# Attention values by 32-column groups, sums from a block of ones, and 1024-column steps on VectorE and ScalarE

## The reference

```python
qh, kh, vh = (split_heads(qp), split_heads(kp), split_heads(vp))
scores = jnp.einsum('bhqd,bhkd->bhqk', qh, kh) * d_head ** (-0.5)
m = mask[:, None, None, :] | causal[None, None, :, :]
scores = scores - m.astype(scores.dtype) * NEG
attn = jax.nn.softmax(scores, axis=-1)
out = jnp.einsum('bhqk,bhkd->bhqd', attn, vh)
out = out.transpose(0, 2, 1, 3).reshape(b, l, d_model)
return out @ Wo.T + bo
```

## Time and profile before

| | us |
|---|---|
| median of 3 runs (763.24 to 767.15) | 765.07 |
| the profiled execution, its own time | 765.94 |
| its span, from the first to the last instruction | 763.8 |
| TensorE busy, of the span | 574.9 |
| VectorE busy | 443.1 |
| ScalarE busy | 407.7 |

### The profile page before, as it was taken

The page is one execution under the profiler, slowest core; times in us unless marked ns, Lnnn a source line. Parts: engine busy times, 40 slices in busy tenths (PEclk is TensorE's granted clock), DMA queues, the critical chain, the costliest instruction groups (busy, mean ns, idle before and its releaser), DMA issues.

```text
span 763.8 us, 14153 instructions
## 1 busy us (share of the span) xinstructions
PE 574.9 (75%) x4326; PEld 405.7 (53%) x4326; DVE 443.1 (58%) x1706; ACT 407.7 (53%) x862; POOL 359.7 (47%) x438
## 2 busy tenths in 40 slices
PE   3499999889888988898898767483778866789800
PEld 1156666556455555555465446362667755679700
DVE  4267788778777877777785773251323322223374
ACT  2257988887787888688786655230322322224300
POOL 4122126644554564455435326647555555550075
PEclk9989999999999999999998987867898999989955
DMA  3363111221122122201111224324544444446498
GB/s 89 71 195 84 45 41 44 61 67 43 50 60 66 29 65 63 66 24 30 38 29 32 83 59 122 105 77 112 158 133 124 118 125 124 120 131 186 133 364 291
DMA packets 74458, 73.59 MB, mean 96 GB/s; under 512 B 22032, under 2 KB 61840, under 8 KB 74096
## 3 DMA queue, kind: packets, MB, share of 16 engines
q1 hardware_dynamic: 64160, 53.86, 26.8%
q0 software_dynamic: 8640, 18.37, 6.8%
q10 hardware_dynamic: 1584, 0.46, 0.2%
HBM read 44.99 MB, written 27.70 MB: 95 GB/s over the span
## 4 chain that ended last, share of the span: by engine, by line
PE 53%; ACT 14%; issue 13%; DVE 7%; another core or an unknown queue 4%; POOL 4%; SPq 2%; DMA 2%; ACTq 0%; POOLq 0%; DVEq 0%
PE bank L638 12%; PE bank L649 10%; PE bank L462 6%; PE bank L484 6%; DVE sm L890 3%; PE bank L466 3%; POOL gathered L1417 3%; PE bank L475 3%; PE bank L629 3%; ACT sm L717 2%; ACT pt L782 2%; ACT vx L709 2%; ACT rows L744 2%; PE bank L491 2%
## 5 line engine op out<-in xcount | busy, mean ns | idle before, releaser
L1354 POOL DMA_INDIRECT routed_rows<-rows,pos x128 | 125.2, 978 | 136.4 <-ACT rows L746 86.2
L1390 POOL DMA_INDIRECT expert_rows_by_token<-yb,token_row x118 | 113.2, 960 | 85.7 <-DVE token_row L1248 40.8
L638 PE MATMUL bank<-xbT,wi 128*128 128x256 f32 x312 | 97.1, 439 | 71.1 <-issue 70.4
L827 ACT ACTIVATE hb<-bank 128x512 f32<-128x512 f32 x78 | 46.6, 597 | 168.7 <-PE bank L638 77.4
L1254 DVE TENSOR_TENSOR yb<-bank,gate 128x256 f32<-128x256 f32 x78 | 33.1, 424 | 172.2 <-PE bank L649 107.2
L638 PEld LDWEIGHTS bank<-xbT,wi 128*128 128x128 f32 x312 | 59.6, 212 | 84.7 <-issue 77.0
L882 DVE TENSOR_REDUCE smax<-bank 128x8 f32<-128x512 f32 x128 | 82.2, 683 | 30.7 <-PE bank L466 25.4
L649 PE MATMUL bank<-wo,hb 128*128 x624 | 91.6, 295 | 0.0
L649 PEld LDWEIGHTS bank<-wo,hb 128*128 128x128 f32 x624 | 85.3, 212 | 0.1
L462 PE MATMUL bank<-kx,qT 64*64 64x512 f32 x512 | 74.6, 654 | 14.0 <-DMA kx<-kT 7.1
L890 DVE TENSOR_TENSOR sm<-bank,smax 128x512 f32<-128x512 f32 x128 | 81.9, 681 | 0.0
(11 more groups left out here) (135 smaller groups left out, 934.8 us busy)
## 6 DMA issues: line engine op xcount, KB each, us to landing
xb<-routed_rows SPq DMA_DIRECT2D x78, 138.0 KB
wi<-w_in SPq DMA_DIRECT2D x78, 128.0 KB
kx<-expert_rows_by_token SPq DMA_DIRECT2D x26, 256.0 KB
ctx_in<-ctx_t SPq DMA_DIRECT2D x16, 256.0 KB
x_all<-x SPq DMA_DIRECT2D x16, 256.0 KB
kx<-kT SPq DMA_DIRECT2D x256, 16.0 KB
out<-x_all SPq DMA_DIRECT2D x16, 256.0 KB
expert_rows<-yb SPq DMA_DIRECT2D x19, 128.0 KB, 2.1
```

Of the source, the lines that this page charges most:

```text
L638: last = nc.tensor.matmul(UBK[b % 2][:, c * BLK:(c + 1) * BLK], wi[:, b % RX, c * P:(c + 1) * P], xbT[:, b % RH, :], start=True, stop=True)
L1354: nc.gpsimd.indirect_dma_start(out=rows_d, out_offset=bass.IndirectOffsetOnAxis(ap=pos[:, buf, k, u:u + 1], axis=0), in_=rows[:, buf, u, : ...
L1390: nc.gpsimd.indirect_dma_start(out=tok_d, out_offset=bass.IndirectOffsetOnAxis(ap=token_row[:, b % RY, u:u + 1], axis=0), in_=yb[:, b % RY ...
```

## The change

Six things change.

1. The products with the values and the sums. The stationary operands are now blocks of 32 columns. For each j in 0, 1 (head pair 2g+j), each sequence b and each g in 0 to 3 one product of a 128x32 block of `vx` with 64 moving columns (the queries of sequence b) adds into partitions 32g to 32g+31, columns 64b to 64b+63 of XB: 16 products a tile. The block has zeros for the heads of the other j, so that the two add up to the attention output with its 128 features on the partitions, which is the form that `project_o` takes. Eight more products of a 128x32 block of ones and zeros with 128 moving columns put each head's sum beside it, repeated over the head's 8 partitions (columns 128 to 255). So a tile has 24 products instead of 8.
2. With that, `queries_to_rows` (4 transposes), `transpose_o` (1 transpose), the evacuation `xo` and the evacuation `onT` go. `normalise(t)` reads XB itself: one reciprocal of 128 columns and one product of 128 columns, written to `onT` (two buffers).
3. `row_maxima`, `subtract_maxima`, `exps` and the evacuation of transposed exponentials are one instruction of 1024 columns each instead of two of 512. The score banks and the probability banks are now two tensors of 1024 columns over two banks each, and `s_sc`, `s_sub`, `s_exp`, `s_pt`, `s_ptev` count once a tile.
4. `values(t)` waits for `normalise(t-1)` (`s_norm`), since that reads XB.
5. `vx` has two buffers, is set to zero at the start (5,120 elements per partition, in place of four copies of 512), and `v_evac(s)` waits for the products of step s-2.
6. The buffer for gathered rows lies in `sm` and has 8 places instead of 6.

```diff
-VM = 64
+VB = 32
-RG = 6
+RG = 8
...
-        vx = sb("vx", [P, U, J, VM])
+        vx = sb("vx", [P, 2, U * J // 2, 2, 2 * VB + 2 * DH])
-        xo = sb("xo", [P, 4, P])
-        rden = sb("rden", [P, J, 2])
-        on = sb("on", [P, D])
-        onT = sb("onT", [P, P])
+        rden = sb("rden", [P, P])
+        onT = sb("onT", [P, 2, P])
...
                     if not first:
-                        pe.wait_ge(s_sub, 2 * t)
+                        pe.wait_ge(s_sub, t)
...
                 def values(t, u):
-                    pe.wait_ge(s_ptev, 2 * t + 2)
-                    for j in range(J):
-                        o = VM * (j % 2)
-                        last = nc.tensor.matmul(XB[o:o + VM, (j // 2) * P:(j // 2 + 1) * P], vx[:, u, j, :],
-                                                pt[:, j, :], start=True, stop=True)
+                    if t:
+                        pe.wait_ge(s_norm, t)
+                    pe.wait_ge(s_ptev, t + 1)
+                    for j in range(2):
+                        for b in range(2):
+                            for g in range(J // 2):
+                                v = vx[:, t // U % 2, u * (J // 2) + g, :, :].rearrange("p a c -> p (a c)")
+                                c = (2 * j + b) * VB
+                                nc.tensor.matmul(XB[g * VB:(g + 1) * VB, b * L:(b + 1) * L], v[:, c:c + VB],
+                                                 pt[:, 2 * g + j, b * L:(b + 1) * L], start=(j == 0 and b == 0), stop=False,
+                                                 skip_group_check=True)
+                    for j in range(2):
+                        for g in range(J // 2):
+                            last = nc.tensor.matmul(XB[g * VB:(g + 1) * VB, P:2 * P],
+                                                    ones_s[:, j * VB:(j + 1) * VB], pt[:, 2 * g + j, :],
+                                                    start=False, stop=(j == 1), skip_group_check=True)
                     last.then_inc(s_pv, 1)
-                def queries_to_rows(t):
...
-                def transpose_o(t):
...
                 def project_o(t):
-                    pe.wait_ge(s_ontev, t + 1)
-                    nc.tensor.matmul(YB[:, P:2 * P], onT[:, :], wo_s[:, :], start=True, stop=True).then_inc(s_y, 1)
+                    if t:
+                        pe.wait_ge(s_res, t)
+                    pe.wait_ge(s_norm, t + 1)
+                    nc.tensor.matmul(YB[:, 0:P], onT[:, t % 2, :], wo_s[:, :], start=True, stop=True).then_inc(s_y, 1)
...
                 def v_evac(s):
                     act.wait_ge(s_v, s + 1)
+                    if runs(s, 2):
+                        act.wait_ge(s_pv, (s - 1) * U)
...
                 def exps(t, u):
-                    for half in range(2):
-                        act.wait_ge(s_sub, 2 * t + half + 1)
-                        heads = sm[:, u % 2, half * HH:(half + 1) * HH, :]
-                        nc.scalar.activation(heads, heads, ACT.Exp).then_inc(s_exp, 1)
+                    act.wait_ge(s_sub, t + 1)
+                    nc.scalar.activation(sm[:, u % 2, :, :], sm[:, u % 2, :, :], ACT.Exp).then_inc(s_exp, 1)
...
                 def row_maxima(t):
+                    dve.wait_ge(s_sc, t + 1)
+                    nc.vector.reduce_max(smax[:, :], S2[:, :].rearrange("p (h k) -> p h k", k=L), AX).then_inc(s_max, 1)
...
                 def normalise(t):
-                    dve.wait_ge(s_tq, t + 1)
-                    y = YB[:, :].rearrange("r (j m) -> r j m", m=VM)
-                    nc.vector.reciprocal(rden[:, :, :], y[:, :, 4 * DH:4 * DH + 2]).then_inc(s_rden, 1)
+                    if t > 1:
+                        dve.wait_ge(s_y, t - 1)
+                    dve.wait_ge(s_pv, t + 1)
+                    nc.vector.reciprocal(rden[:, :], XB[:, P:2 * P]).then_inc(s_rden, 1)
                     dve.wait_ge(s_rden, t + 1)
-                    for b in range(2):
...
+                    nc.vector.tensor_tensor(onT[:, t % 2, :], XB[:, 0:P], rden[:, :], ALU.mult).then_inc(s_norm, 1)
...
-                for u in range(U):
-                    last = nc.vector.tensor_copy(vx[:, u, :, :], ones_s[:, :].unsqueeze(1).broadcast_to([P, J, VM]))
-                last.then_inc(s_zero, 1)
+                nc.vector.memset(vx[:, :, :, :, :], 0.0).then_inc(s_zero, 1)
```

122 lines of the change are left out of this document (43 added, 79 removed).

## The result

The changed kernel takes 796.5 us (median, 793.87 to 799.14) against 764.2 us (762.14 to 767.15) for the kernel before: a ratio of 1.044, 95% interval 1.040 to 1.049. The forecast was 750 us and faster; the range ended at 782. The profiled execution has a span of 794.9 us, against 763.8.

The account below looks back on a forecast made before the run. No engine was full; VectorE's and TensorE's rings were near the bound, VectorE last after the change. Savings of 0.9 us a step, 14.4 for 16 steps, 16.4 with the end, took 765.94 to 749.5, about 750 us; range 731 to 782.

Parts of the forecast that it names:

- the stall at u = 0: VectorE's 2.85 us idle before the residual ending u = 0: taken as external and staying, with 0.55 us a step saved there.
- VectorE's ring: Residual, subtraction, normalisation, small work, next maxima: +0.27 us a tile plus 0.05 handoff; last at u = 1, 2, level at u = 3.
- No dearer than the 1.02 before: Products with the values on TensorE: 48 records, four at once, taken as 1.05 us a tile against 1.02 before.
- Rival 3: Values on TensorE: the 48 records don't run four at once, 1.68 or 3.06 us; about 781 or 870 us; chance 0.17.
- the added wait: TensorE's values waiting for the previous tile's normalisation: 0 to 0.2 us, with slack for VectorE at u = 1 and 2.
- 0.9 us in each of 16 steps: Attention part: 0.35 us from three turns plus 0.55 at u = 0, 14.4 us in all; 16.4 with the end.
- The reciprocal: Normalisation on VectorE: a 128-column reciprocal taken as 1.0 us, making normalisation 1.33 us, 0.45 more a tile.
- rival 1: Normalisation: the reciprocal is as cheap as a product (0.29 us), TensorE's ring sets all turns; about 736 us; chance 0.16.
- Maxima and differences: VectorE's instructions of 1024 columns: 1.20 us each against 1.29 for two halves, saving 0.18 us a tile in all.
- The windows: Residual-to-residual turns of one attention step of four tiles, 25.8 us, to become 24.9; VectorE idle 0.55 us at u = 1.
- VectorE is last: Attention turns: VectorE sets the pace at u = 1 and 2 and is level at u = 3, saving 0.35 us together.
- the sign that would refute the prediction: Before VectorE's residuals: idle time there would show the forecast wrong; none was expected at u = 1, 2, 3.

Follow-up runs that it names:

- e5: The changed kernel with all eight scatters of a step waiting behind the output projections (three after u = 0, three after u = 1, two after u = 2): 736.6 us, ratio 0.954.
- e6: The kernel before with all eight scatters of a step moved behind the output projections, as in e5: 750.7 us, ratio 0.972.
- e9: e5 with two small VectorE routing steps rewritten (product L915 on ScalarE, copy L921 as a maximum over one element): 722.6 us, ratio 0.947.
- e10: e5 with the reciprocal computing 16 of 128 columns from the second tile on, output wrongly scaled: 721.3 us, ratio 0.944.
- e2: The kernel before with each product with the values cut into two of 64 columns, 32 records instead of 16, scatters in old places: 796.8 us, ratio 1.042.
- e4: The changed kernel with the scatter pairs of u = 1 and u = 2 waiting for that turn's output projection: 768.4 us, ratio 1.004.
- e11: The kernel before with every second product with the values cut into two of 64 columns, 24 records, scatters in old places: 784.2 us, ratio 1.029.

## Why the prediction was wrong

**Where it failed.** The step is the sentence on the stall at u = 0: "I take the stall to come from outside the five engines' work, and to stay." It came from one of the five, GpSimd, and it was not fixed to that turn: it belongs to scatters that meet a group of many short TensorE records. The rows for it were at hand: VectorE waited long after the recorded end of what it waited for, and GpSimd's four scatters filled the same 5 us. I looked at the DMA share of the window and didn't ask what GpSimd did. Had I, the next question would have been what stands beside the pairs at u = 1 and u = 2: the values, whose records the change triples. In the sum this is the term that stood at nothing: VectorE's ring has no idle time before the residuals at u = 1, 2 and 3, and the changed kernel waits there 1.17, 1.83 and 0.99 us on average.

**The values, priced right and still the cause.** "No dearer than the 1.02 before" holds: 1.02 from the first record to the projection. Rival 3 had the right place and sign with the wrong mechanism. The group doesn't take longer on TensorE; its notice comes 2 us later. In the sum this term had a width of 0 to 0.2 us a turn (the added wait) where u = 2 lost 1.65 in the sampled step and 1.40 on average.

**The rest of the sum,** with the holds gone (e5 against e6): 14.2 us saved, 16.4 predicted. That they are so close is mostly luck. The prediction put 0.9 us in each of 16 steps; over the 13 steps e5 saves 0.16 each. By the spans, of 12.8 us saved 7.1 lie ahead of the first expert product (427.5 against 434.6 us) and 5.7 behind it, where the prediction had nothing. In both kernels the stretched instructions of the routing lie over the comparison.
- The reciprocal took 939 ns, taken as 1.0 us; rival 1 (290) is out. The line through two small widths in the earlier trace rows was good to 7%.
- Maxima and differences took 1217 and 1218 ns, predicted 1.20 us.
- VectorE a step: 21.18 us busy in the changed kernel, 21.8 by the prediction's terms (20.7 and four times 0.27).
- The windows: one step of 25.81 us stood for all. The mean of the 13 steps is 26.75, with 6.70 instead of 5.32 at u = 1, so VectorE's idle time there was read too small (0.55, on average 1.08).
- "VectorE is last": wrong in the changed kernel, where it waits 94 us before its residuals. In e5 it fills three turns, but with 2.3 us a step of stretching that the prediction didn't have; in e9, with most of that gone, it waits 0.72 and 0.52 us on average at u = 2 and u = 1. I had named idle time there as the sign that would refute the prediction.
- The stall at u = 0 stayed, as expected, with 2.61 in place of 2.85. The 0.55 counted there came out as 0.07.
- e10 shows that VectorE's and TensorE's rings are closer together than my windows had them: 0.7 us less for each tile gives only 7 us.

**The size of the loss.** In the sampled step u = 1 and u = 2 lost 2.96 us and the others won 0.26, but the 1.31 of u = 1 is a matter of which step was sampled. On average u = 2 lost 1.40, u = 0 0.87, u = 3 0.57 and u = 1 0.36. The loss at u = 3 goes with the clock: its six turns at full clock take 5.78 on average, its seven others 6.96. An estimate from these turns, place by place: the changed kernel's turns below full clock are together some 25 us longer than as many at full clock, those of the kernel before some 8. So at most some 17 of the 32 us are the clock's. e2 loses as much with almost the clock of the kernel before; it has the holds and none of the change's savings.

Against a kernel that has the change without holds (e5), the changed one stands 9.5% higher (1.044 over 0.954). Of that, 5.2% (1.004 over 0.954) goes with the four scatters of u = 0, which stall the kernel before as well, and 4.0% (1.044 over 1.004) with the two pairs. The pair at u = 2 hardly stalls the kernel before (idle 0.53 us on average), that at u = 1 does (1.08). The first share has the clock in it: 18 turns are below full clock in e4 and 4 in e5.

**What stays open.** The runs show that the hold at u = 2 needs both scatters and a group of many short records, and grows with both. With the four scatters of u = 0, 16 records are enough. At u = 1 the dose isn't shown: the kernel before waits 1.08 us there with 16 records (0.67 in e6, its scatters moved), and e11, e2 and the changed kernel little more (1.34, 1.22 and 1.17). Why a notice is late isn't shown. Nor was it tried whether the number of records or their rate counts, or whether it is the products or their weight loads. Why the clock was lower in the changed kernel isn't shown either: it came back to 0.97 when the scatters were moved (e5), which fits a clock that fell because TensorE was held up, and no run tests that.

## What to carry to other kernels

Where an engine goes on long after the recorded end of what it waited for, list what every other engine issues in that stretch before calling the stall external, and look first for GpSimd's indirect DMAs. Take windows over several steps before one stands for all, and read the granted clock of each. Before cutting a TensorE group into more and shorter products, see which scatters run beside it: to move them behind the group's consumer cost three waits and was worth more (2.8% in the kernel before, 8.6% in the changed one) than the change itself (1.9%). See then what comes behind them on GpSimd: its products may now stand beside VectorE's instructions on SBUF. A change that meets such a stall is priced once more in a version without it, or its worth is read with the wrong sign.

## What the runs showed of the hardware

- TensorE's notices are held while GpSimd issues indirect DMAs beside a group of many short products, about 2 us with two scatters and 32 or 48 records. The Trainium skill's "SBUF — State Buffer" (Who interferes with whom) says that PE and ACT never wait on anyone; for an access to SBUF that may be so, but in these runs the notices do wait.
- A VectorE product with both operands in SBUF, and a copy from SBUF to SBUF, are stretched by a GpSimd product of 512 columns with both operands in SBUF, and end with it. L915 took 192 ns in the changed kernel and this in e5:

```profile
215.83 1.58 DVE L915 TENSOR_TENSOR probs<-ex,r_inv 128x32 f32<-128x32 f32 x1
216.07 1.28 POOL L1284 TENSOR_TENSOR x_all<-x_all,cvec 128x512 f32<-128x512 f32 x1
```

The two ends are 217.41 and 217.35. An indirect DMA alone beside it left it at 0.19 us (at 471.29 us in e5). The same section of the Trainium skill says that a VectorE instruction with two SBUF inputs, or a copy in a mode with two ports, contends with a GpSimd instruction that reads SBUF, and that a reduction doesn't. For the product the trace agrees, with 1.58 us beside GpSimd's product and 0.19 without. The maximum that took the copy's place in e9 took 162 ns, but ended before GpSimd's product began, so no run here shows the part on the reduction.
- A reciprocal of 128 columns took 939 ns, 3.2 times a product of the same width (291).
- 48 records with 32-column weights, four column groups side by side, took 1.02 us, as long as 16 records with 64-column weights.
